# Two cross-attention layers on one core: queries in two buffers, and six units of the order moved

## The reference

```python
# layer 0: 8 heads of width 40, keys from the context without its last 4 rows (371)
hs    = mha(x @ Wq, enc @ Wk, enc @ Wv)
ca_q1 = einsum('btc,th->bch', ca, Wq_ca)[:, indices, :]        # the last 4 rows of the context
ca_h1 = mha(ca_q1, x, x)
ca_h2 = mha(ca_h1 @ Wq, ca @ Wk_ca, ca @ Wv_ca)
x1    = (hs + ca_h2) @ Wout + b_out + x
# layer 1: 20 heads of width 16, keys from all 375 rows of the context
out   = mha(x1 @ Wq, ctx @ Wk, ctx @ Wv) @ Wo + bo + x1
```

## Time and profile before

| | |
|---|---|
| median of 3 runs | 742.46 us (741.77 to 744.25) |
| profiled execution | 742.2 us, of which the span is 740.4 |
| TensorE matmul busy | 697.9 us, 94% |
| TensorE weight load busy | 613.4 us, 83% |
| VectorE busy | 467.7 us, 63% |
| ScalarE busy | 404.1 us, 55% |
| GpSimd busy | 294.9 us, 40% |
| granted TensorE clock over the run | 0.978 |
| share of the chain that ended last | PE 74%, DVE 9%, ACT 8% |

### The profile page before, as it was taken

How to read it: one execution, slowest core, us unless ns; L and a number is a source line. 1 busy time by engine, 2 the same in 40 slices (tenths; PEclk the granted TensorE clock), 3 DMA queues, 4 the chain that set the end, 5 groups by cost and what they waited for, 6 DMA issues and landing times.

```text
span 740.4 us, 18130 instructions
## 1 busy us (share of the span) xinstructions
PE 697.9 (94%) x6924; PEld 613.4 (83%) x6924; DVE 467.7 (63%) x996; ACT 404.1 (55%) x923; POOL 294.9 (40%) x401
## 2 busy tenths in 40 slices
PE   8887999999999999999999999999999999999975
PEld 5576888888888888888888888888888888888864
DVE  2553665757567675757577575756767575767661
ACT  2555555655565555655655565556555565564431
POOL 5484662453335253433426345323525443321200
PEclk9879999999999999999999999999999999999995
DMA  9533544342615344252524434261533425060400
GB/s 328 173 104 87 124 118 93 86 100 64 144 51 141 74 112 99 67 127 53 138 62 125 96 83 103 66 141 50 140 75 102 107 70 129 18 143 19 83 9 9
DMA packets 52387, 72.45 MB, mean 98 GB/s; under 512 B 12128, under 2 KB 44256, under 8 KB 52304
## 3 DMA queue, kind: packets, MB, share of 16 engines
q1 hardware_dynamic: 44832, 60.34, 31.9%
q0 software_dynamic: 6144, 9.25, 6.5%
q10 hardware_dynamic: 1328, 1.71, 0.6%
HBM read 20.60 MB, written 4.26 MB: 34 GB/s over the span
## 4 chain that ended last, share of the span: by engine, by line
PE 74%; DVE 9%; ACT 8%; issue 3%; POOL 1%; DMA 0%; ACTq 0%; POOLq 0%
PE bankX L1017 29%; PE bankO L1239 9%; PE bankST L1205 7%; PE bankS L1171 6%; PE bankST L1199 5%; ACT arena L608 3%; ACT arena L590 2%; DVE negmax L786 2%; PE bankX L1099 2%; PE bankX L1130 2%; PE bankX L1137 2%; PE bankS L1168 2%; DVE qn L778 2%; PE bankX L1090 2%; PE bankX L1145 1%
## 5 line engine op out<-in xcount | busy, mean ns | idle before, releaser
L786 DVE TENSOR_REDUCE negmax<-bankS 112x2 f32<-112x750 f32 (+1 forms) x224 | 208.7, 932 | 38.9 <-PE bankS L1171 22.0
L507 POOL DMA_DIRECT2D k_stack<-stage x192 | 96.2, 509 | 180.6 <-DVE stage L821 153.6
L590 ACT ACTIVATE arena<-bankST 125x1344 f32<-125x1344 f32 x80 | 103.5, 1293 | 33.0 <-PE bankST L1205 33.0
L1239 PE MATMUL bankO<-arena,v 125*32 125x112 f32 (+2 forms) x2688 | 101.9, 265 | 5.6 <-ACT arena L590 3.0
L1239 PEld LDWEIGHTS bankO<-arena,v 125*32 125x32 f32 (+2 forms) x2688 | 83.5, 118 | 21.7 <-issue 20.0
L1171 PE MATMUL bankS<-k_stack,q1T 112*112 112x376 f32 x320 | 87.5, 355 | 3.3 <-DVE negmax L786 2.8
L1017 PE MATMUL bankX<-ctx_hi,WH 128*120 128x376 f32 (+2 forms) x192 | 69.1, 360 | 2.5 <-DVE qn L778 2.2
L1017 PE MATMUL bankX<-WH,ctx_hi 128*125 128x320 f32 x192 | 66.7, 347 | 2.4 <-DVE qn L778 2.4
L470 POOL TENSOR_TENSOR w2bd<-w2s,cst 96x896 fp32r<-96x896 f32 x16 | 29.9, 1869 | 95.9 <-DVE w2s L778 95.9
L1205 PE MATMUL bankST<-q1T,k_stack 112*125 112x224 f32 x480 | 66.8, 276 | 1.2 <-DMA q1T<-mT 1.2
L1205 PEld LDWEIGHTS bankST<-q1T,k_stack 112*125 112x125 f32 x480 | 63.3, 192 | 2.3 <-DMA q1T<-mT 1.5
(11 more groups left out here) (141 smaller groups left out, 1518.0 us busy)
## 6 DMA issues: line engine op xcount, KB each, us to landing
k_stack<-stage SPq DMA_DIRECT2D x96, 176.2 KB
k_stack<-stage SPq DMA_DIRECT2D x192, 70.5 KB, 2.6
k_stack<-stage POOLq DMA_DIRECT2D x192, 47.0 KB, 2.0
ctx_raw<-in_ctxT SPq DMA_DIRECT2D x16, 376.0 KB, 3.2
k_stack<-stage SPq DMA_DIRECT2D x48, 117.5 KB
xp<-in_xpad SPq DMA_DIRECT2D x16, 224.0 KB, 3.3
x_raw<-in_xT SPq DMA_DIRECT2D x16, 168.0 KB, 2.4
out<-x1b SPq DMA_DIRECT2D x16, 140.0 KB, 3.3
```

The costliest lines, as they stand in the source:

```text
L507: pool.dma_start(dst, src).then_inc(k1_stacked_pool[b % 2], 16)
L590: nc.scalar.activation(dst[0:KC], bankST[0:KC, :, 0:GROUP * SQ], ACT.Exp).then_inc(exp_done, 1)
L786: nc.vector.tensor_reduce(negmax[:, n % 2, 2 * pair:2 * pair + 2], bankS[0:SQ, :, 0:keys], axis=AX, op=ALU.max, negate=True).then_inc(max_ ...
L1239: last = nc.tensor.matmul(dst, v, src[0:keys, c, SQ * j:SQ * j + SQ], start=(c == 0), stop=(c == NKC - 1))
```

## The change

There are four edits.

1. The query buffer `qn` becomes `q0n` for layer 0 and `q1n` for layer 1. `hn0` and `hn1` become one `hn`, `caT_sb` moves into `o1T`, and `MT_BUFS` goes from 4 to 2, which makes the room in SBUF.
2. `q1T_2` moves from phase 1 of slot 1 to phase 1 of slot 4, ahead of `out1`. `N1a` moves from phase 3 of slot 1 into the place it leaves.
3. `V0_0` moves from slot 5 to slot 4, `V0_1` from slot 6 to slot 5, `V0_2` from phase 3 of slot 6 to phase 0. `T2_0` moves from the end of slot 5 into phase 1 of slot 6, just ahead of `T2_1`.
4. In the first slot alone the reciprocal of the tokens' sums comes right after the first maximum on VectorE.

```diff
-MT_BUFS = 4
+MT_BUFS = 2
...
     ([("V1_0", -1)], [("q1T_0", -1)], [("V1_1", -1)], [("W2", 1), ("PV2", 0)]),
-    ([("q1T_1", -1), ("V1_2", -1)], [("q1T_2", -1)], [("q0", 1)], [("N1a", -2), ("K1_0", 0)]),
+    ([("q1T_1", -1), ("V1_2", -1)], [("N1a", -2)], [("q0", 1)], [("K1_0", 0)]),
     ([("K1_1", 0)], [("S3", 0), ("S2_0", 1)], [("N1b", -2)], [("S2_1", 1)]),
     ([("K1_2", 0)], [("K0_0", 1)], [("hn1T", -2)], [("K0_1", 1)]),
-    ([("K0_2", 1)], [("out1", -2)], [("p3T", 0), ("N0", 0)], [("q0T_0", 1)]),
-    ([("hn0T", 0), ("V0_0", 1)], [("q0T_1", 1)], [("out0", 0)], [("T2_0", 1)]),
-    ([("x1T", 0), ("V0_1", 1)], [("T2_1", 1)], [("q1", 0)], [("V0_2", 1)]),
+    ([("K0_2", 1), ("V0_0", 1)], [("q1T_2", -1), ("out1", -2)], [("p3T", 0), ("N0", 0)], [("q0T_0", 1)]),
+    ([("hn0T", 0), ("V0_1", 1)], [("q0T_1", 1)], [("out0", 0)], []),
+    ([("x1T", 0), ("V0_2", 1)], [("T2_0", 1), ("T2_1", 1)], [("q1", 0)], []),
...
-        qn = sb("qn", [SQ, H1 * 64], F32R)
+        q0n = sb("q0n", [SQ, H0 * 120], F32R)
+        q1n = sb("q1n", [SQ, H1 * 64], F32R)
...
-        hn0 = sb("hn0", [SQ, HID])
-        hn1 = sb("hn1", [SQ, HID])
+        hn = sb("hn", [SQ, HID])
...
-        caT_sb = sb("caT_sb", [P, 2, B * NTOK])
...
+        caT_sb = o1T[:, 0:2, 0:B * NTOK]
...
+                    if (t, i) == (0, 0):
+                        reciprocal2(0)
                     if before:
                         copy_mT(before)
...
-                    if (t, i) == (0, 0):
-                        reciprocal2(0)
```

More of the change, by code:

```diff
@@ L507, in stack_k1 @@
                         pool.dma_start(dst, src).then_inc(k1_stacked_pool[b % 2], 16)
-            nc.gpsimd.memset(qn[:, :].bitcast(F32), 0.0).then_inc(zeroed, 1)
+            nc.gpsimd.memset(q1n[:, :].bitcast(F32), 0.0).then_inc(zeroed, 1)
             nc.gpsimd.memset(k0_stack[:, :, :].bitcast(F32), 1.0).then_inc(zeroed, 1)
@@ L656, in unit @@
                 elif kind == "q0":
-                    if b == 0:
-                        act.wait_ge(zeroed, 1)
-                    dst = qn[:, 0:H0 * 120].rearrange("p (h a d) -> p h a d", h=H0, a=3)[:, :, 0:3:2, :]
+                    dst = q0n[:, :].rearrange("p (h a d) -> p h a d", h=H0, a=3)[:, :, 0:3:2, :]
                     src = X[0:SQ, 0:HID].rearrange("p (h d) -> p h d", h=H0).unsqueeze(2)
@@ L663, in unit @@
                 elif kind == "q1":
-                    dst = qn[:, :].rearrange("p (h a d) -> p h a d", h=H1, a=4)[:, :, 0:3:2, :]
+                    if b == 0:
+                        act.wait_ge(zeroed, 1)
+                    dst = q1n[:, :].rearrange("p (h a d) -> p h a d", h=H1, a=4)[:, :, 0:3:2, :]
                     src = X[0:SQ, 0:HID].rearrange("p (h d) -> p h d", h=H1).unsqueeze(2)
@@ L829, in unit @@
                     dve.wait_ge(q0_rounded, b + 1)
-                    parts = qn[:, 0:H0 * 120].rearrange("p (h a d) -> p h a d", h=H0, a=3)
+                    parts = q0n[:, :].rearrange("p (h a d) -> p h a d", h=H0, a=3)
                     scaled_lo(parts[:, :, 1, :], X[0:SQ, 0:HID].rearrange("p (h d) -> p h d", h=H0), SCALE0,
@@ L834, in unit @@
                     dve.wait_ge(q1_rounded, b + 1)
-                    parts = qn[:, :].rearrange("p (h a d) -> p h a d", h=H1, a=4)
+                    parts = q1n[:, :].rearrange("p (h a d) -> p h a d", h=H1, a=4)
                     scaled_lo(parts[:, :, 1, :], X[0:SQ, 0:HID].rearrange("p (h d) -> p h d", h=H1), SCALE1,
@@ L861, in unit @@
                 elif kind == "N0":
-                    normalised(name, b, hn0[:, :], X, H0, 64, D0, r0[:, :], hn0_ready)
+                    normalised(name, b, hn[:, :], X, H0, 64, D0, r0[:, :], hn0_ready)
                 elif kind == "N1a":
-                    normalised(name, b, hn1[:, 0:16 * D1], X, 16, 32, D1, r1[:, 0:16], hn1_ready)
+                    normalised(name, b, hn[:, 0:16 * D1], X, 16, 32, D1, r1[:, 0:16], hn1_ready)
                 elif kind == "N1b":
-                    normalised(name, b, hn1[:, 16 * D1:HID], X, 4, 32, D1, r1[:, 16:20], hn1_ready)
+                    normalised(name, b, hn[:, 16 * D1:HID], X, 4, 32, D1, r1[:, 16:20], hn1_ready)
                 elif kind == "out0":
@@ L963, in warm_up @@
                 pe.wait_ge(zeroed, 1)
-                zeros = qn[:, 0:512].bitcast(F32)
+                zeros = q1n[:, 0:512].bitcast(F32)
                 for _ in range(4):
@@ L1083, in unit @@
                         last = nc.tensor.transpose(X[0:120, h * SQ:h * SQ + SQ],
-                                                   qn[:, c:c + 120].bitcast(F32), ident[0:SQ, 0:SQ])
+                                                   q0n[:, c:c + 120].bitcast(F32), ident[0:SQ, 0:SQ])
                 elif kind == "q1T":
@@ L1090, in unit @@
                         last = nc.tensor.transpose(X[:, g * SQ:g * SQ + SQ],
-                                                   qn[:, c:c + 128].bitcast(F32), ident[0:SQ, 0:SQ])
+                                                   q1n[:, c:c + 128].bitcast(F32), ident[0:SQ, 0:SQ])
                 elif kind in ("hn0T", "hn1T", "x1T"):
-                    src, of = {"hn0T": (hn0, "N0"), "hn1T": (hn1, "N1b"), "x1T": (x1, "out0")}[kind]
+                    src, of = {"hn0T": (hn, "N0"), "hn1T": (hn, "N1b"), "x1T": (x1, "out0")}[kind]
                     pe.wait_ge(bank_drained[bank(of, b)], drained(of, b))
```

## The result

The changed kernel takes 751.5 us (median of 4 runs, 750.82 to 755.75) where the kernel before takes 742.33 (741.77 to 744.25): a ratio of 1.0114, with a 95% interval of 1.0073 to 1.0154. The forecast was 750.6 us, slower. The profiled execution after took 751.5 us with a span of 749.7, against 742.2 and 740.4.

A forecast was written before the change was run, and what follows sets the result against it. TensorE's queue was taken to set the time. Waits made less waits ended gave 0.55 us per iteration, 0.6 with small things, times 14 is 8.4 us on 742.2: 750.6 us, range 747 to 754.5 (8 in 10).

The forecast's parts named there:

- four marks: Trace signs: 0.8 us wait before `q1`; late `p3T` and `N0` in slot 4; L778 waits gone; iterations 0.6 us longer.
- S + 3.3: Slot 4: `N0` starts 3.3 us after S, the start of the shifted scores, where before it was 2.67.
- the two `T2` together: Slot 6: `q1` takes the bank of `T2_0`, whose ScalarE copy stands behind the exponentials, and waits: +0.81 us per iteration.
- `V0` a place sooner: Slots 4 to 0: `V0_0` starts later, +0.11 us, and `V1_0` no longer waits for `q1`'s drain, -0.32 us.
- small things: Effects not priced singly, such as slot 0's first maximum behind a later `q1`: 0 to 0.1 us per iteration, half taken.
- `V0_0` a place sooner: Slot 4: `V0_0` follows `K0_2` directly and waits for VectorE to drain `K0_1`: +0.11 us per iteration.
- `q1T_2` ahead of `out1`: Slot 4: VectorE's half of `q1T_2` delays `out1`'s addition, `N0` and the second maximum: +0.48 us beyond the moved work.
- What the change ends: Old TensorE waits vanish per iteration: `V0_1` -0.20 us, `V1_0` in slot 0 -0.32, `K1_0` in slot 1 -0.33.
- At no cost: Separate query buffers remove no wait, other buffers resize no instruction; the first slot's early reciprocal gives 0 to -0.5 us once.
- slot 4's delay is swallowed: Rival: slot 4's 0.48 and 0.11 us fall away, the sum is -0.04 and the time 742 us; chance 0.08.
- `q1` doesn't wait: Rival: in slot 6 the bank is free before TensorE reaches `q1`, so 738.6 us; chance 0.04.
- The falling clock: Rival: TensorE's clock falls in the new waits, losing 1.6 us each; 773 us, or 755 to 760; chance 0.07.

The follow-up runs named there:

- e5: The changed kernel with the first slot's reciprocal back where it was before the change: 751.89 us, ratio 1.0098 to the kernel before.
- e1: The changed kernel with `T2_0` back at the end of slot 5: 744.32 us, ratio 1.0010 to the kernel before.
- e2: The changed kernel with `q1T_2` and `N1a` back at their old places in slot 1: 751.01 us, ratio 1.0112 to the kernel before.
- e8: The kernel before with only the order of `V0` changed, a place sooner: 740.37 us, ratio 0.9959 to the kernel before.
- e3: The changed kernel with `q1T_2` and `out1` exchanged in slot 4: 750.81 us, ratio 1.0107 to the kernel before.
- f3: The changed kernel with `q1T_2` moved from slot 4 to behind `K1_1` in slot 2: 747.38 us, ratio 1.0057 to the kernel before.
- e4: The changed kernel with the old table of units, so only buffers and the first slot's reciprocal stay changed: 744.76 us, ratio 1.0013 to the kernel before.
- f1: The changed kernel with `q1T_2` behind `K1_1` in slot 2, `T2_0` back in slot 5 and the reciprocal late: 738.46 us, ratio 0.9941 to the kernel before.

## Why the prediction was right, step by step

The range and the side were right. All the four marks that it named for the trace are there: the wait before `q1` released by L687, `N0` at S + 3.3, the L778 waits gone, and 0.62 us per iteration for a forecast 0.6. The granted clock of this kernel was 1.00 in each 10 us between 100 and 690 us. (One window over the whole stretch would not have told: `e5`'s reads 1.00 too, with its fall inside.) No new wait stands in slots 2, 3 or 5.

The sum was made of three moves, and each was measured by a kernel with it undone or done alone:

| part | predicted, us | measured, us |
|---|---|---|
| the two `T2` together (0.81 - 0.20) | 0.61 | 0.64 (changed less `e1`) |
| `q1T_2` to slot 4, `N1a` sooner (0.48 - 0.33) | 0.15 | 0.09 (changed less `e2`) |
| `V0` a place sooner (0.11 - 0.32) | -0.21 | -0.08 (`e8` less before) |
| together | 0.55 | 0.62 (changed less before) |

That the total came out to 0.02 us is in part luck. Part of the measured 0.64 and -0.08 is a cost in slot 0 that none of the three terms holds. From the transpose of the maxima (L1184) there to the one in slot 1 the kernels take 6.81 us before, 6.89 in `e8`, 6.91 in `e1` and 7.03 in the changed kernel (means of eleven iterations). Without its 0.12 and 0.08 the three moves come to 0.52 + 0.09 - 0.16 = 0.45 us, where the sum had 0.55. Slot 0 costs about 0.2 in place of the 0.05 that was put on the small things, and fills the gap.

*`V0_0` a place sooner.* Right in kind: it waits for `K0_1`. The step from `K0_2` to the shifted scores grew by 0.15 us, with the slower first matmul.

*`q1T_2` ahead of `out1`.* The chain was right to 0.02 us at each of its places (the end of VectorE's half, `p3T`, `N0`, `hn0T`). That neither `out1`'s addition nor `V0_0` is at fault is shown by `e3` and `f3`.

*The two `T2`.* The wait before `q1` was put at 0.81 us and is 0.73. The bank is free when predicted (S + 2.63); TensorE reaches `q1` 0.07 us later, since eight transposes in a row take 0.74 us up to the next scores.

*What the change ends.* The waits of `V0_1`, `V1_0` and `K1_0` are gone. `V1_0`'s -0.32 was measured as -0.33 in its own place, but the mis-sized term is what the units behind give back. `V0_2` no longer stands between `q1` and slot 0's first scores, so VectorE's remainder of `q1` now holds up the first maximum there, and the second scores wait for that maximum: 0.07 us later in `e8`, 0.19 us in the changed kernel (1.24 us after the shifted scores; before 1.05). The prediction had this as one of its small things of 0 to 0.1.

*At no cost.* `e4` confirms it of the buffers, in the middle of the run. It is not so for the reciprocal. It was put down at 0 to -0.5 us, and in seven executions the start is 1.0 us longer with it in the mean, with the clock at 0.50 for 3.4 us more (under `e5`). The prediction had left the clock out of this term.

*The ends of the run.* The prediction took 14 equal iterations and nearly nothing beside them. Here the two profiled executions are cut at the transpose of the maxima (L1184) in slot 0, where both kernels have done the same units:

| stretch | before, us | changed, us | more, us |
|---|---|---|---|
| start to slot 0 of iteration 1 | 80.17 | 80.85 | 0.68 |
| iteration 1 | 40.69 | 41.92 | 1.23 |
| iterations 2 to 14 | 549.78 | 557.89 | 8.11 |
| iteration 15 to the end | 69.76 | 69.04 | -0.72 |
| span | 740.4 | 749.7 | 9.3 |

Thirteen iterations cost 0.62 us each. Iteration 1 costs 0.6 us more than that (the 1.37 us wait of `N0`), the first stretch, with the first wait before `q1`, 0.68, and the end gives 0.72 back. Beyond the thirteen that leaves 0.57 us (0.68 + 0.61 - 0.72), about the 0.6 us of a fourteenth iteration, which was luck. The shorter end was not tested. The clock falls there at other moments from run to run, and that stretch lies between 67.3 and 72.2 us over all the profiled kernels, so its cause stays open.

*The rivals.* That slot 4's delay is swallowed is excluded by `f3`, and that `q1` doesn't wait by `e1`. The falling clock is excluded for the middle iterations of the changed kernel by the windows of 10 us, and happened once, in iteration 1 of `e5`.

## What to carry to other kernels

With two banks in turn, a unit's place has two prices: when its own drain comes, and whose bank the unit two places on then takes. So read the drain's engine queue and look for what long instruction stands ahead of it there. The `T2` copy behind 1.3 us of exponentials holds nobody up where the eight matmuls of `q1` lie between it and the next taker of its bank, and costs 0.73 us where only a second `T2` and a pair's scores do. Whether such a copy can stand ahead of the exponentials instead is worth a try: `f1` did it for `q1T_2`. Buffers that permit a move bring nothing by themselves: with the same two query buffers one order is 1.1% slower than the kernel before, one is 0.6% slower (`f3`, where only `q1T_2` stands elsewhere), and one 0.6% faster (`f1`, where `T2_0` is back in slot 5 too). And read the first maximum of the next slot as one more term: it was the cost that the sum had left to the small things.

## What the runs showed of the hardware

The same wait can be followed by a fall of TensorE's clock or by none. The 1.37 us wait of iteration 1 was followed by one in `e5` (granted 0.54 over 3.4 us) and by none in the changed kernel, `e1` and `e3`. The 0.83 us wait of the earlier trace rows was followed by one in the kernel before (granted 0.59), and the same wait in the changed kernel by none:

```profile
52.24 0.45 PE L1123 MATMUL bankX<-w2bd,ca_st 96*112 96x448 f32 x1 [0.83 <-DVE stage L821]
```

```profile
51.50:55.50 4.00, 2.76 (x29) 2.12 (x30) 3.15 (x11) 3.00 (x14) 0.17 (x1) 1.00 0.03 7
```

So the length of a wait alone doesn't say whether the clock falls.

A start that comes sooner can end later. In the changed kernel `T2` began 2.6 us sooner than before, and a wait of 2.03 us opened behind it. The granted clock stayed at 0.50 until 45.2 us, where before it was back at 42.0. In the four executions with that earlier `T2` and that wait the clock was low for 13.6 to 13.7 us at a stretch, in three without them for 10.2, and the first `p3T` came 1.0 us later in the mean.
